# Cross-attention on one core: score maxima and masked image scores read over two PSUM banks at once

## What is computed

```python
q = split_heads(x @ w_q, 20)
k, v = split_heads(text @ w_k, 20), split_heads(text @ w_v, 20)
out_text = merge(softmax(q @ k.T / sqrt(16)) @ v)
k_ip, v_ip = split_heads(ip @ w_k_ip, 20), split_heads(ip @ w_v_ip, 20)
out_ip = merge(softmax(q @ k_ip.T / sqrt(16) + mask_ip) @ v_ip)   # mask from boxes: 0 or -10000
out = (out_text + out_ip) @ w_out + b_out + x
```

## Time and profile before

| | us |
|---|---|
| median of 3 runs | 246.53 |
| lowest and highest run | 244.32, 246.85 |
| the profiled execution | 243.46 |
| its span, first to last instruction | 241.5 |
| TensorE matmul / weight load busy | 191.8 / 156.7 |
| VectorE / ScalarE / GpSimd busy | 166.2 / 127.3 / 90.8 |

### The profile page before, as it was taken

The page is one execution under the profiler, slowest core; times in us unless marked ns, Lnnn a source line. Parts: engine busy times, 40 slices in busy tenths (PEclk is TensorE's granted clock), DMA queues, the critical chain, the costliest instruction groups (busy, mean ns, idle before and its releaser), DMA issues.

```text
span 241.5 us, 4536 instructions
## 1 busy us (share of the span) xinstructions
PE 191.8 (79%) x1608; PEld 156.7 (65%) x1608; DVE 166.2 (69%) x375; ACT 127.3 (53%) x289; POOL 90.8 (38%) x99
## 2 busy tenths in 40 slices
PE   0799999794897509986989699959869974998962
PEld 0699999793864408665767578747657754775741
DVE  0679893557267145985797598859867875879593
ACT  4554852223394234934784387359347732767750
POOL 6021220004420780548063726544482332645320
PEclk9999999996799955999799979999997995899999
DMA  6998369975877594169429843963594295011111
GB/s 210 381 323 297 120 181 181 262 249 111 277 182 199 165 171 142 65 153 216 125 71 190 185 138 98 203 174 133 129 180 125 78 196 103 4 57 64 54 57 54
DMA packets 34213, 38.04 MB, mean 157 GB/s; under 512 B 10096, under 2 KB 31344, under 8 KB 34032
## 3 DMA queue, kind: packets, MB, share of 16 engines
q1 hardware_dynamic: 34192, 37.76, 60.0%
HBM read 25.96 MB, written 11.80 MB: 156 GB/s over the span
## 4 chain that ended last, share of the span: by engine, by line
DMA 34%; PE 32%; DVE 14%; SPq 10%; issue 4%; ACT 3%; POOL 1%; DVEq 0%; POOLq 0%
PE bank L419 12%; DMA key_w<-shift_dram 9%; DMA q_dram<-q_l 8%; DMA qs<-shift_dram 8%; DVE negmax L1002 7%; PE bank L511 6%; PE bank L488 5%; SPq L287 4%; SPq L303 3%; PE bank L524 3%; PE bank L552 3%; PE bank L566 3%; DMA vip_dram<-vipn 2%; DMA shift_dram<-shift 2%; DMA ks<-k_dram 2%
## 5 line engine op out<-in xcount | busy, mean ns | idle before, releaser
L1002 DVE TENSOR_REDUCE negmax<-bank 128x4 f32<-128x448 f32 x80 | 49.8, 622 | 30.9 <-PE bank L488 30.5
L792 ACT ACTIVATE raw<-bank 112x512 f32<-112x512 f32 x80 | 45.9, 601 | 24.1 <-PE bank L511 23.8
L1153 POOL TENSOR_TENSOR x_l<-x_raw,x_h 128x512 fp32r<-128x512 f32 x8 | 11.1, 1390 | 61.8 <-ACT x_h L735 61.8
L511 PE MATMUL bank<-key_w 100*112 100x256 f32 x80 | 18.3, 326 | 13.8 <-DMA key_w<-shift_dram 13.8
L511 PE MATMUL bank<-qs,ks 100*112 100x256 f32 x80 | 17.5, 307 | 9.9 <-DMA qs<-shift_dram 9.4
L511 PEld LDWEIGHTS bank<-key_w 100*112 100x112 f32 x80 | 13.3, 208 | 15.6 <-DMA key_w<-shift_dram 14.8
L552 PE MATMUL bank<-raw,v 112*32 112x256 f32 x320 | 22.4, 387 | 1.3 <-DVE late L1045 0.8
L419 PE MATMUL bank<-ctx_hl,key_w 128*128 128x448 f32 x72 | 17.2, 403 | 7.4 <-DVE ctx_hl L930 7.4
L566 PE MATMUL bank<-raw,con 112*32 112x256 f32 x320 | 22.1, 382 | 0.0
L1204 POOL TENSOR_TENSOR late<-late 128x256 f32<-128x256 f32 x20 | 14.6, 729 | 19.8 <-DVE late L1045 19.8
L419 PE MATMUL bank<-wo_h,ctx_hl 128*128 128x320 f32 x80 | 19.7, 317 | 2.8 <-DVE ctx_hl L930 1.8
(11 more groups left out here) (102 smaller groups left out, 475.5 us busy)
## 6 DMA issues: line engine op xcount, KB each, us to landing
qs<-q_dram SPq DMA_DIRECT2D x12, 320.0 KB, 5.1
key_w<-q_dram SPq DMA_DIRECT2D x12, 320.0 KB, 5.1
x_raw<-xT SPq DMA_DIRECT2D x8, 384.0 KB, 7.2
q_dram<-q_h SPq DMA_DIRECT2D x8, 384.0 KB, 3.8
q_dram<-q_l SPq DMA_DIRECT2D x8, 384.0 KB, 2.7
late<-x SPq DMA_DIRECT2D x8, 320.0 KB, 3.2
out<-late SPq DMA_DIRECT2D x8, 320.0 KB, 6.4
ks<-k_dram SPq DMA_DIRECT2D x24, 75.0 KB, 3.3
```

Of the source, the lines that this page charges most:

```text
L511: mm = pe.matmul(banks[p % len(banks)][0:TEXT, S * ab:S * ab + S], ks[k][0:STACK + SHIFT, p, ab, 0:TEXT], qs[k][0:STACK + SHIFT, p, :], st ...
L792: nc.scalar.activation(probs[:, p, :], b_banks(b)[p % len(b_banks(b))][0:TEXT, :], ACT.Exp, scale=SCALE).then_inc(p_done, 1)
L1002: nc.vector.tensor_reduce(negmax[:, t, :, 2 * g:2 * g + 2].rearrange("p a q -> p q a"), s[:, :, 0:TEXT].rearrange("p (q a) n -> p q a n", ...
L1153: sub = lambda o, a, b: nc.gpsimd.tensor_tensor(o, a, b, ALU.subtract)
```

## The change

The two "a" banks become one tile `a_pair` of two banks, one for each `t`. A turn is now a group `g` for both `t`: four matmuls, then one reduction and one add over both banks. There are five turns instead of ten. With one tile there is no second buffer: `score_a(g)` waits until the add of the group before is done, and the read of group `g` waits for its four matmuls. TensorE's and VectorE's orders are written anew; `low_q` 1 now stands behind the read of group 2, and `low_ip` 1 ahead of the read of group 1.

```diff
-        bank = [ctx.enter_context(nc.psum_tensor(f"bank{i}", [P, 512], F32)) for i in range(8)]
+        a_pair = ctx.enter_context(nc.psum_tensor("a_pair", [P, QT, 512], F32))
+        bank = [a_pair[:, t] for t in range(QT)]
+        bank += [ctx.enter_context(nc.psum_tensor(f"bank{i}", [P, 512], F32)) for i in range(QT, 8)]
...
-            def score_a(c, k, n):
-                if n == 0:
+            def score_a(c, k, g):
+                if g == 0:
                     pe.wait_ge(qs_in, 16 * 3 * (c + 1))
                     pe.wait_ge(ks_in, 16 * 6 * (c + 1))
-                t, g = n // GROUPS, n % GROUPS
-                if n >= 2 or not (isinstance(c, int) and c == 0):
-                    pe.wait_ge(a_used, 2 * GROUPS * c + n - 1)
-                for p in range(2):
-                    mm = pe.matmul(a_bank[n % 2][:, 2 * KEYS * p:2 * KEYS * (p + 1)],
+                if c or g:
+                    pe.wait_ge(a_used, GROUPS * c + g)
+                for t in range(QT):
+                    for p in range(2):
+                        mm = pe.matmul(a_pair[:, t, 2 * KEYS * p:2 * KEYS * (p + 1)],
...
                 mm.then_inc(a_ready, 1)
...
                 if not exists(b - 1):
-                    more_a(2)
+                    group(0)
                     pe.wait_ge(sl_done, c)
                     project_q(b + 2)
                     transpose_ip(b, k, 0)
                     transpose_ip(b, k, 1)
-                    more_a(2)
-                    for p in range(4):
-                        score_b(b, k, p)
+                    group(1)
+                    pairs(0, 4)
                 else:
                     score_b(b, k, 0)
...
                     if exists(b + 2):
-                        more_a(1)
-                        both(1)
+                        group(0)
+                        score_b(b, k, 1)
                         transpose_ip(b, k, 0)
                         transpose_ip(b, k, 1)
-                        both(2)
-                        both(3)
+                        group(1)
+                        pairs(2, 4)
...
-                both(4)
+                group(2)
+                score_b(b, k, 4)
                 text_out(b, k, 0)
-                both(5)
+                score_b(b, k, 5)
+                group(3)
                 text_sums(b, k, 0)
-                both(6)
+                score_b(b, k, 6)
                 if exists(b + 2):
                     pe.wait_ge(ql_done, 2 * (b + 3))
                 image_out(b, 0)
-                both(7)
+                score_b(b, k, 7)
+                group(4)
                 image_out(b, 1)
-                both(8)
-                both(9)
+                pairs(8, 10)
...
-            for n in range(2 * GROUPS):
-                score_a(0, 0, n)
-                if n % 2 and n < 8:
-                    project_v(4 + n // 2)
+            for g in range(GROUPS):
+                score_a(0, 0, g)
+                if g < 4:
+                    project_v(4 + g)
...
-            def read_a(c, n):
-                t, g = n // GROUPS, n % GROUPS
+            def read_a(c, g):
                 heads = slice(GROUP * g, GROUP * (g + 1))
-                dve.wait_ge(a_ready, 2 * GROUPS * c + n + 1)
+                dve.wait_ge(a_ready, GROUPS * c + g + 1)
...
-                s = a_bank[n % 2][:, 0:GROUP * KEYS].rearrange("p (h n) -> p h n", h=GROUP)
-                nc.vector.tensor_reduce(negmax[:, t, :, 2 * g:2 * g + 2].rearrange("p a q -> p q a"),
-                                        s[:, :, 0:TEXT].rearrange("p (q a) n -> p q a n", a=2), X, ALU.max,
+                scores = a_pair[:, :, 0:GROUP * KEYS].rearrange("p t (h n) -> p t h n", h=GROUP)
+                nc.vector.tensor_reduce(negmax[:, :, :, 2 * g:2 * g + 2],
+                                        scores[:, :, :, 0:TEXT].rearrange("p t (q a) n -> p t a q n", a=2), X, ALU.max,
                                         negate=True).then_inc(a_max, 1)
-                nc.vector.tensor_tensor(ips[:, t, heads, :], s[:, :, TEXT:KEYS],
-                                        mask[:, t, c, :].unsqueeze(1).to_broadcast([P, GROUP, IP]),
+                nc.vector.tensor_tensor(ips[:, :, heads, :], scores[:, :, :, TEXT:KEYS],
+                                        mask[:, :, c, :].unsqueeze(2).to_broadcast([P, QT, GROUP, IP]),
                                         ALU.add).then_inc(a_used, 1)
...
-                some_a(2)
+                if exists(c):
+                    read_a(c, 0)
                 low_ip(b, k, 0)
-                some_a(1)
                 low_ip(b, k, 1)
-                some_a(1)
+                if exists(c):
+                    read_a(c, 1)
                 if exists(b + 2):
                     low_q(b + 2, 0)
+                if exists(c):
+                    read_a(c, 2)
+                if exists(b + 2):
                     low_q(b + 2, 1)
-                some_a(1)
...
                 if exists(b - 1):
                     last_chunk_out(b - 1)
-                some_a(5)
                 if exists(c):
+                    read_a(c, 3)
+                    read_a(c, 4)
```

More of the change, by code:

```diff
@@ L476, in project_v @@
                        for t, w in ((ctx_h, wv_h), (ctx_h, wv_l), (ctx_l, wv_h))]).then_inc(va_ready, 1)
[L478 to L480 removed]
+            def score_a(c, k, g):
+                if g == 0:
                     pe.wait_ge(qs_in, 16 * 3 * (c + 1))
                     pe.wait_ge(ks_in, 16 * 6 * (c + 1))
[L483 to L491 removed]
+                if c or g:
[3 more added lines that the diff above has]
+                        mm = pe.matmul(a_pair[:, t, 2 * KEYS * p:2 * KEYS * (p + 1)],
+                                       qs[k][0:STACK, 2 * g + p, t * P:(t + 1) * P],
+                                       ks[k][0:STACK, 2 * g + p, :, :].rearrange("p a n -> p (a n)"),
+                                       start=True, stop=True)
                 mm.then_inc(a_ready, 1)
             def transpose_max(c):
[L495 removed]
+                pe.wait_ge(a_max, GROUPS * (c + 1))
                 for t in range(QT):
@@ L593, in step, with group, pairs @@
                     project_q(b + 2)
[L594 to L600, removed]
-                    more_a(1)
-                    score_b(b, k, p)
+                def group(g):
+                    score_a(c, 1 - k, g)
+                def pairs(first, end):
+                    for p in range(first, end):
+                        score_b(b, k, p)
                 if not exists(b - 1):
-                    more_a(2)
+                    group(0)
                     pe.wait_ge(sl_done, c)
@@ L623, in step @@
                     if exists(b + 2):
-                        more_a(1)
-                        both(1)
+                        group(0)
+                        score_b(b, k, 1)
                         transpose_ip(b, k, 0)
                         transpose_ip(b, k, 1)
-                        both(2)
-                        both(3)
+                        group(1)
+                        pairs(2, 4)
                     elif exists(c):
                         score_b(b, k, 1)
-                        more_a(2)
+                        group(0)
                         transpose_ip(b, k, 0)
                         transpose_ip(b, k, 1)
-                        both(2)
-                        both(3)
-                    else:
-                        for p in (1, 2, 3):
-                            score_b(b, k, p)
+                        group(1)
+                        pairs(2, 4)
+                    else:
+                        pairs(1, 4)
                         transpose_ip(b, k, 0)
@@ L1074, in step @@
                 c = b + 1
-                reads = [n for n in range(2 * GROUPS) if exists(c)]
-                def some_a(n):
-                    for _ in range(n):
-                        if reads:
-                            read_a(c, reads.pop(0))
                 if not exists(c):
@@ L1138, in _ @@
             low_q(1, 1)
-            for n in range(2 * GROUPS):
-                read_a(0, n)
+            for g in range(GROUPS):
+                read_a(0, g)
             image_max(0)
```

4 lines of the change are left out of this document (2 added, 2 removed).

## The result

Over four runs each the median went from 245.43 us (243.41 to 246.85) to 269.63 us (265.31 to 273.47). The ratio is 1.089, 95% interval 1.069 to 1.108. Forecast were 253.8 us and a range that ended at 260.

What follows compares the result with a forecast made beforehand. No engine fills the span: each step is a loop of shifts, scores, maxima and a DRAM round trip. Hand-over delays of 1.3 + 5 x 1.2 = 7.3 us on the 246.53 us median gave 253.8 us, range 249.3 to 260.

Steps and rivals of the forecast that it cites:

- The two gaps: TensorE's waits for VectorE's adds before groups 1 and 2 of a step: 0.4 to 0.7 and 1.25 us.
- the sums: TensorE's work after the text output and group 3; forecast to start 1.54 us late in step 4.
- b9: Tenth "b" score pair of a step; key loads and shift store follow it, 1.3 us late in step 4.
- landing: Arrival of a step's new shifts through DRAM, 6.49 us after their store is issued in step 4.
- the sum's treatment of the clock: Adding up the steps: 1.3 us for fully clocked step 4, 1.2 each for five others, 7.3 us in all.
- the first gap of a cold step: Wait before group 1 when the clock starts low: covered by slower image transposes, taking 0.7 us off the lower bound.
- Rival C: New gaps early in each step also cost clock, 1 us a step in six steps: 259.8 us, chance 0.10.
- Step 4 kept its clock after 2.25 us: Argument against gaps costing clock: in the old kernel's profile, step 4 ran at the high clock throughout.
- A hand-over without a second buffer: At the shared tile, each group's matmuls wait for the previous add, and everything behind them on TensorE waits too.
- Rival A: VectorE's instruction count decides and hand-overs fall into TensorE's idle time: 3.6 us saved, 242.9 us, chance 0.05.
- Rival B: Transfers set the steps and hide the delay, so step length doesn't grow: 246.5 to 248 us, chance 0.07.
- the ring: One step's loop: shifts land, TensorE scores, VectorE takes maxima, these are transposed, new shifts return through DRAM; 21.7 us.

Runs made afterwards that it cites:

- experiment 10: Changed kernel with one-bank reads, one hand-over of both banks, and idle-time matmuls ahead of the shifts and in the two gaps: 251.5 us, ratio 1.027.
- experiment 4: Changed kernel with idle-time matmuls ahead of the wait for the shifts and before groups 1 and 2 of each step: 247.8 us, ratio 1.017.
- experiment 6: Kernel of before with idle-time matmuls ahead of the wait for the shifts: 240.7 us, ratio 0.981.
- experiment 5: Changed kernel with idle-time matmuls only before groups 1 and 2 of each step, none ahead of the shifts: 255.1 us, ratio 1.048.
- experiment 3: Changed kernel with idle-time matmuls only ahead of the wait for the shifts: 259.4 us (252.9 to 263.3).
- experiment 8: Kernel of before, third and fifth "a" turn of steps 0 to 6 waiting for the add of the turn just before: 264.9 us, ratio 1.094.
- experiment 1: Changed kernel's order of work, each bank read by its own instructions and handed over by itself: 265.9 us (258.0 to 267.9).
- experiment 9: Changed kernel's order with one-bank reads handed over bank by bank, plus idle-time matmuls ahead of the shifts and in the gaps: 248.3 us, ratio 1.014.
- experiment 12: Kernel of before with idle-time matmuls ahead of the shifts and its ten interleaved turns taken group by group: 238.8 us, ratio 0.981.
- experiment 7: Kernel of before with each "a" turn waiting for the add of the turn just before it: 291.2 us, ratio 1.187.

## Why the prediction was wrong, step by step

**Right, by the traces.** Sign and direct cost. The reduction at 1.09 us (1.10). The wide read's gain of 0.12 a group (experiment 10, on the path twice). The two gaps, 0.42 and 1.13 (0.4 to 0.7 and 1.25). With the clock held, in experiment 4, the sums at 7.34 (7.22), b9 at 10.82 (10.80), maxima transposed at 11.29 (11.27), and the whole 7 to 8 us (7.3). b9 did decide, by the key loads, and the way from store to landing stayed at 9.9 us (9.5 in experiment 4). In steps 1 and 3 of the changed kernel itself, where the clock came back as before, the price was 1.0 us a step (1.2). The step of 23.0 us was 22.7 to 22.9 where the clock held.

**The step that failed** is the sum's treatment of the clock: I took the clock of every step over from before: high throughout in step 4, and in the others low at the start and then back, which made the price 1.2 us a step. No profiled step of the changed kernel kept the clock from landing to the maxima, and in steps 2, 4, 5 and 6 it ran at half for long stretches behind the first 4 us, where before it had come back. That the first gap of a cold step is covered was right: in step 4 it had shrunk to 0.14 us and the second to 0.46, and yet the clock stayed low. The gaps cost clock beyond their own length. In step 4 the sums were 2.4 and b9 4.3 late against the same step with the gaps filled (15.1 against 10.8), over three times the direct 1.3 of a step. Of the 24 us, some 7 are direct (experiments 4 and 6). The changed kernel loses 269.6 - 247.8 = 22 us to the clock and the kernel of before 245.8 - 240.7 = 5, so the remaining 17 are lost clock.

**Rival C** had named this mechanism with a chance of 0.10 and a price of 6 us, from 2 us of TensorE's work a step at half speed, half of it showing. What went wrong there is the duration: I let the clock come back after 2 us of work. In step 4 it stayed low nearly to the maxima, and in steps 5 and 6 likewise, and the text output and the sums of the first chunk ran in that stretch; they are on the path to b9, so their stretching shows in full. That the gaps keep it low experiment 5 shows; why gaps of 0.14 and 0.46 us do, with TensorE busy 6.54 of 7 us by the records, no run here tells. "Step 4 kept its clock after 2.25 us" was an argument from one step of a kernel that had a single idle time of 0.48 us behind its landing. The Trainium skill has a rule that I should have weighed, in TensorE: Matmul & The Clock Gate, section on a second failure mode: a kernel that cycles through PSUM banks can idle so often for a moment between groups of matmuls that its clock goes up and down, at a cost in throughput. Experiments 3 and 8 agree with it. Experiment 3 answers my argument: of five steps with a full-clock start and gaps behind it three lost the clock, and with the gaps filled (experiment 4) none of them did. The sign that I had named for C, a clock below 0.9 in the first 5 us of most steps, could tell nothing: in the kernel of before the first 4 us already had 0.50, 0.57, 0.61, 1.00, 0.67 and 0.50 in steps 1 to 6. The sign that would have told is the 7 us behind them. The forecast of some 10 us of TensorE's idle time for the adds was off too: it was 5.2; in step 4 slower rows filled most of the gaps.

**My name for the direct cost** was too narrow. "A hand-over without a second buffer" is what TensorE waits for, but with two buffers and the same order of work (experiments 1 and 9) the time hardly moves: the read of group 1 waits for both image parts either way. The placing of the work, which one shared tile forces, is what the turns of experiment 12 do without. How much a second buffer alone would give in this placing, with neither fillers nor a lost clock, stays open: experiment 1 had lost its clock, and in experiment 9 the fillers occupy the gap.

**Rivals A and B** fell. The text output came 6.3 after the landing in step 4, not 4.0 or earlier, and the ring grew with b9.

## What to carry to other kernels

Before giving up a ping-pong of two buffers for wider instructions, lay the new order over one step and look for places where TensorE has nothing to do. Price such a gap twice: by its length, and by what the rest of the step costs at half clock, since the second may be the larger by far. It needn't strike in every step or every run. Where a wait is unavoidable, matmuls into a bank that is about to be overwritten can hold the clock: they made the kernel of before 2% faster and took 22 us off the changed one. The other way is to alternate the work finely enough that there is no gap.

## What the runs showed of the hardware

Idle times of 0.4 and 1.1 us behind a start at full clock brought TensorE to 0.55 to 0.59 for the next 7 us in three steps of one execution and left it at 1.00 in two others (experiment 3); with the same places filled it stayed at 1.00 in all five (experiment 4; in step 6 only the second place is filled). The start of a step and its middle act separately: fillers ahead of the shifts gave the first 4 us a full clock but not always the rest, fillers in the gaps gave it to the rest but not to the first 4 us (0.57, experiment 5). And runs of one program differ with the clock: the changed kernel's four were in the order of their mean clocks (265.3 us at 0.855, 268.7 at 0.844, 270.5 at 0.832, 273.5 at 0.816), and so were experiment 3's, from 252.9 at 0.951 to 263.3 at 0.894. A clock that isn't held needn't make them spread: experiments 5 and 7 lay within 1.2%.
